# Attention with relative positions: sums over keys left of the query moved from TensorE to ScalarE and GpSimd

## The reference, cut

```python
xn = layernorm(x)                          # x: (2, 2048, 256)
q, k, v = proj(Wq, bq), proj(Wk, bk), proj(Wv, bv)      # 16 heads of 16
idx = clip(r[None, :] - r[:, None], -128, 128) + 128
scores = (einsum('bhqd,bhkd->bhqk', q, k) + einsum('bhqd,qkd->bhqk', q, rel_k[idx])) / sqrt(16)
w = softmax(scores, axis=-1)
s = (einsum('bhqk,bhkd->bhqd', w, v) + einsum('bhqk,qkd->bhqd', w, rel_v[idx])) @ Wo.T + bo
logits = xn @ Wg + bg                      # 8 experts, the best one per token
y = gelu(xn @ W1[e]) @ W2[e]               # e = argmax(logits)
out = x + s * silu(y)
```

## Time and profile before

| | |
|---|---|
| median of three runs | 2635.67 us (2635.24 to 2641.53) |
| profiled execution, its own time | 2641.73 us |
| its span | 2640.0 us |
| TensorE matmul busy | 2420.9 us (92%) |
| VectorE busy | 1828.1 us (69%) |
| ScalarE busy | 1749.4 us (66%) |
| GpSimd busy | 884.5 us (34%) |
| mean granted TensorE clock | 0.973 |

### The profile page before, as it was taken

The page is one execution under the profiler, slowest core; times in us unless marked ns, Lnnn a source line. Parts: engine busy times, 40 slices in busy tenths (PEclk is TensorE's granted clock), DMA queues, the critical chain, the costliest instruction groups (busy, mean ns, idle before and its releaser), DMA issues. The chain is left out here.

```text
span 2640.0 us, 47807 instructions
## 1 busy us (share of the span) xinstructions
PE 2420.9 (92%) x15216; PEld 1184.1 (45%) x15216; DVE 1828.1 (69%) x4985; ACT 1749.4 (66%) x4026; POOL 884.5 (34%) x1977
## 2 busy tenths in 40 slices
PE   6838999999999999999999999999999999799998
PEld 3412444444444444444444444444444444567666
DVE  6558777777777777777777777777777774233333
ACT  4514877777777777777777777777777777321121
POOL 1222454333333333333333333333333332133332
PEclk9955999999999999999999999999999999999999
DMA  5668889777777777777777777777777762642221
GB/s 160 176 141 265 244 268 243 235 222 230 233 230 237 225 222 233 234 231 236 232 228 234 231 236 236 231 226 226 233 231 238 227 194 88 244 144 69 66 64 53
DMA packets 351151, 541.00 MB, mean 205 GB/s; under 512 B 30608, under 2 KB 259392, under 8 KB 350912
## 3 DMA queue, kind: packets, MB, share of 16 engines
q1 hardware_dynamic: 336880, 502.76, 61.8%
q0 software_dynamic: 14032, 35.24, 4.5%
HBM read 272.60 MB, written 269.43 MB: 205 GB/s over the span
## 5 line engine op out<-in xcount | busy, mean ns | idle before, releaser
L1073 DVE TENSOR_REDUCE part<-ps 128x1 f32<-128x512 f32 (+3 forms) x2048 | 1189.5, 591 | 457.8 <-PE ps L957 438.8
L1135 ACT ACTIVATE probs_T<-pst 128x512 f32<-128x512 f32 (+3 forms) x2048 | 985.3, 525 | 397.4 <-PE pst L966 390.0
L957 PE MATMUL ps<-k_front,q_front 96*128 96x512 bf16 x2048 | 790.1, 393 | 13.0 <-DVE part L1071 2.5
L915 PE MATMUL pout<-probs_T,v_far 128*32 128x512 f32 (+3 forms) x4864 | 550.8, 533 | 40.4 <-ACT probs_T L1111 31.4
L822 POOL TENSOR_TENSOR left_T<-probs_T,left_mask 128x128 f32<-128x128 f32 x512 | 219.5, 429 | 991.7 <-ACT probs_T L1111 797.4
L957 PEld LDWEIGHTS ps<-k_front,q_front 96*128 96x128 bf16 x2048 | 198.6, 97 | 587.8 <-DVE part L1073 296.8
L966 PE MATMUL pst<-q_back,k_left 102*128 102x512 bf16 (+3 forms) x1024 | 349.7, 343 | 0.7 <-ACT probs_T L1135 0.6
L966 PE MATMUL pst<-q_back,k_right 102*128 102x512 bf16 (+3 forms) x1024 | 348.8, 342 | 0.5
L1148 ACT ACTIVATE band<-band,negm 128x384 f32<-128x384 f32 (+1 forms) x512 | 305.5, 597 | 0.1
L1071 DVE CUSTOM_DVE_ANT_0 band<-ps,band 128x256 f32<-128x256 f32 (+2 forms) x704 | 300.5, 427 | 0.0
L915 PEld LDWEIGHTS pout<-probs_T,v_far 128*32 128x32 f32 x4864 | 174.5, 108 | 237.9 <-issue 211.4
(11 more groups left out here) (160 smaller groups left out, 2112.0 us busy)
## 6 DMA issues: line engine op xcount, KB each, us to landing
rel_scores<-rel SPq DMA_DIRECT2D x128, 1024.0 KB, 7.9
band_probs<-band SPq DMA_DIRECT2D x128, 768.0 KB, 3.9
pwin<-band_probs SPq DMA_DIRECT2D x128, 512.0 KB
band<-rel_scores SPq DMA_DIRECT2D x64, 768.0 KB
band<-rel_scores SPq DMA_DIRECT2D x64, 576.0 KB, 5.2
w<-in_w_dram SPq DMA_DIRECT2D x16, 1024.0 KB, 14.3
band<-rel_scores SPq DMA_DIRECT2D x64, 128.0 KB, 5.7
q_terms<-terms SPq DMA_DIRECT2D x48, 128.0 KB
```

The source lines that it names most:

```text
L915: return nc.tensor.matmul(pout[32 * g:32 * g + 32, c0:c1], values, probs, start=first, stop=False, skip_group_check=True)
L957: nc.tensor.matmul(ps1[u % 2][:, :], q_front[a.par][:, a.s * P:(a.s + 1) * P], k_front[a.par][:, u * CW:(u + 1) * CW], start=True, stop=Tr ...
L1073: ins = nc.vector.tensor_reduce(peak, src, AX_X, ALU.max)
L1135: ins = nc.scalar.activation(probs_T[t.s % 2][:, u * CW + c0:u * CW + c1], pst[u % 2][:, c0:c1], ACT.Exp, scale=SCALE)
```

## The change

The sum over keys left of the query within its own block needs no product on TensorE: it is the sum of a masked row times one vector. The new kernel takes the diagonal block of `band`, with queries on partitions, masks it on GpSimd (lag 6), sums each row on ScalarE with a copy that accumulates (lag 7, at the step's end), multiplies the 16 sums of a pair by `rv_left` on GpSimd, and VectorE adds the product before the division. `left_T`, `left_values` and `all_pv` go. The shift rows are turned by VectorE in blocks of 32x32 into `shT` (lag 5, behind tile u=3) and placed into `q_back` by four copies on GpSimd; TensorE's transposes and ScalarE's copy go. The slots' indirect transfers move to the last 16 steps of the last head, two a step, and SP reads the table behind its loop.

```diff
-        left_T = sb("left_T", [P, NB, P], F32)
...
+        left = two("left", [P, P], F32)
+        left_sum = two("left_sum", [P, NB], F32)
+        left_part = two("left_part", [P, NB, HD], F32)
...
+        shb = two("shb", [P, CH, 32], BF16)
+        shT = sb("shT", [P, CH, 32], BF16)
...
-                    if hb == 2 and off == 2:
-                        sp.wait_ge(slots_filled, 16 * TILES)
-                        sp.dma_start(slots[:, :, :], dram["slots"].rearrange("(t p) k -> p t k", p=P)).then_inc(slots_in, 16)
...
+                sp.wait_ge(slots_filled, 16 * TILES)
+                sp.dma_start(slots[:, :, :], dram["slots"].rearrange("(t p) k -> p t k", p=P)).then_inc(slots_in, 16)
...
+                    q = Step(hb, off - 6)
+                    if off % CH == 2 and q.valid:
+                        pool.wait_ge(rows_tp, q.count(4, q.r + 1))
+                        if q.r == 0:
+                            wait(pool, st_mm, q.count(64, -64))
...
+                        summed = Step(hb, off - 7)
+                        if summed.valid:
+                            pool.wait_ge(left_ready, summed.count(16, summed.s + 1))
...
+                        rows = q_back[q.par][ROWS:ALLROWS, q.r * CW:(q.r + 1) * CW].rearrange("p (g b c) -> p b g c", g=CH, b=P // 32)
+                        for b in range(P // 32):
+                            if b > 0:
+                                pool.wait_ge(rows_link, q.count(12, 3 * q.r + b))
+                            ins = nc.gpsimd.tensor_copy(rows[:, b], shT[32 * b:32 * b + SHIFTS, :, :])
+                            ins.then_inc(rows_link if b < P // 32 - 1 else rows_copied, 1)
+                        pool.wait_ge(rows_copied, q.count(4, q.r + 1))
...
+                    w = Step(hb, off - 6)
...
-                        pool.wait_ge(bandT_evac, w.count(16, w.s + 1))
-                        if w.s == 0:
-                            wait(pool, all_pv, w.count(1, 0))
-                        own = probs_T[w.s % 2][:, w.s * P:(w.s + 1) * P]
-                        nc.gpsimd.tensor_tensor(left_T[:, w.s, :], own, left_mask[:, :], ALU.mult).then_inc(left_ready, 1)
+                        pool.wait_ge(band_ready, w.count(16, w.s + 1))
+                        own = band[w.par][:, w.s, P:2 * P]
+                        wait(pool, left_sums, w.count(16, w.s - 1))
+                        nc.gpsimd.tensor_tensor(left[w.s % 2][:, :], own, left_mask[:, :], ALU.mult).then_inc(left_ready, 1)
...
+                    ended = Step(hb, off - 8)
+                    if ended.valid and ended.s == NB - 1:
+                        pool.wait_ge(left_sums, ended.count(16, 16))
+                        wait(pool, norm_done, ended.count(1, -1))
+                        nc.gpsimd.tensor_tensor(left_part[ended.par][:, :, :], left_sum[ended.par][:, :].unsqueeze(2).to_broadcast([P, NB, HD]),
+                                                rv_left[:, :].unsqueeze(1).to_broadcast([P, NB, HD]), ALU.mult).then_inc(left_done, 1)
...
+                    first = 2 * NB + 3
+                    if at_end(hb) and first <= off < first + TILES // 2:
+                        if off == first:
                             pool.wait_ge(slots_set, 16)
-                        pool.indirect_dma_start(out=dram["slots"][:, :], out_offset=bass.IndirectOffsetOnAxis(ap=pos_i[:, off:off + 1], axis=0),
-                                                in_=tok_i[:, off, :], in_offset=None).then_inc(slots_filled, 16)
+                        for k in range(2):
+                            i = 2 * (off - first) + k
+                            pool.indirect_dma_start(out=dram["slots"][:, :], out_offset=bass.IndirectOffsetOnAxis(ap=pos_i[:, i:i + 1], axis=0),
+                                                    in_=tok_i[:, i, :], in_offset=None).then_inc(slots_filled, 16)
...
-                        pe.wait_ge(shift_ready, y.count(4, y.r + 1))
-                        wait(pe, rows_copied, y.count(4, y.r))
-                        if w.valid:
-                            wait(pe, winT_evac, w.count(16, w.s + 1))
-                        for g in range(CH):
-                            mm = nc.tensor.transpose(prow[0:SHIFTS, g * P:(g + 1) * P], shb[y.r % 2][:, g, :], con["ident_bf"][:, :])
-                        mm.then_inc(rows_tp, 1)
...
-                    def left_values():
-                        for g in range(CH):
-                            mm = weighted(g, 0, CW, rv_left[:, :], left_T[:, CH * g:CH * g + CH, :].rearrange("p i c -> p (i c)"))
-                        return mm
...
-                        if u == 0 and ended.s == NB - 1 and ended.valid:
-                            pe.wait_ge(left_ready, ended.count(16, 16))
-                            left_values().then_inc(all_pv, 1)
...
-                        if u == 1 and off % CH == 2 and y.valid:
-                            shift_rows()
...
-                        if off % CH == 2 and y.valid:
-                            pe.wait_ge(rows_copied, y.count(4, y.r + 1))
...
+                    def shift_rows():
+                        dve.wait_ge(shift_ready, shifted.count(4, shifted.r + 1))
+                        wait(dve, rows_copied, shifted.count(4, shifted.r))
+                        nc.vector.transpose(shT[:, :, :].rearrange("p g k -> p (g k)"), shb[shifted.r % 2][:, :, :].rearrange("p g k -> p (g k)")).then_inc(rows_tp, 1)
...
+                        if u == CH - 1 and off % CH == 1 and shifted.valid:
+                            shift_rows()
...
-                        dve.wait_ge(den_ready, o.count(1, 1))
                         dst = attn[:, o.n, :, :].rearrange("p (g r) d -> p r g d", g=CH)
-                        nc.vector.tensor_tensor(dst, back[:, :, :, 0:HD], rv.unsqueeze(3).to_broadcast([P, CH, CH, HD]), ALU.mult).then_inc(norm_done, 1)
+                        dve.wait_ge(left_done, o.count(1, 1))
+                        nc.vector.tensor_tensor(dst, back[:, :, :, 0:HD], left_part[o.par][:, :, :].rearrange("p (g r) d -> p r g d", g=CH),
+                                                ALU.add).then_inc(den_ready, 1)
+                        dve.wait_ge(den_ready, o.count(2, 2))
+                        nc.vector.tensor_tensor(dst, dst, rv.unsqueeze(3).to_broadcast([P, CH, CH, HD]), ALU.mult).then_inc(norm_done, 1)
...
-                        act.wait_ge(all_pv, ended.count(1, 1))
+                        act.wait_ge(near_pv, ended.count(2, 2))
...
-                    def shift_rows():
-                        act.wait_ge(rows_tp, shifted.count(4, shifted.r + 1))
-                        nc.scalar.activation(q_back[shifted.par][ROWS:ALLROWS, shifted.r * CW:(shifted.r + 1) * CW], prow, ACT.Copy).then_inc(rows_copied, 1)
...
-                        wait(act, left_ready, t.count(16, t.s - 1))
...
-                        if u == 1 and off % CH == 2 and shifted.valid:
-                            shift_rows()
...
+                    masked = Step(hb, off - 7)
+                    if masked.valid:
+                        act.wait_ge(left_ready, masked.count(16, masked.s + 1))
+                        if masked.s == 0:
+                            wait(act, left_done, masked.count(1, -1))
+                        own = left[masked.s % 2][:, :]
+                        nc.scalar.activation(own, own, ACT.Copy, accum_out=left_sum[masked.par][:, masked.s:masked.s + 1]).then_inc(left_sums, 1)
```

More of the change, by code:

```diff
@@ L555, in attend @@
         rv_win = sb("rv_win", [P, 2, 32], F32)
-        rv_left = sb("rv_left", [P, 32], F32)
+        rv_left = sb("rv_left", [P, HD], F32)
         part = sb("part", [P, NB, 3, CH], F32)
@@ L563, in attend @@
         sh = sb("sh", [P, CH, 2], F32)
-        shb = two("shb", [P, CH, SHIFTS], BF16)
+        shb = two("shb", [P, CH, 32], BF16)
+        shT = sb("shT", [P, CH, 32], BF16)
         rden = sb("rden", [P, NB], F32)
@@ L605, in attend @@
         rows_tp = sem("rows_tp")
+        rows_link = sem("rows_link")
         rows_copied = sem("rows_copied")
@@ L618, in attend @@
         near_pv = sem("near_pv")
-        all_pv = sem("all_pv")
+        left_sums = sem("left_sums")
+        left_done = sem("left_done")
         out_evac = sem("out_evac")
@@ L683, in near_columns @@
             return bl[0] * P, (bl[-1] + 1) * P
-        CONSTS = 18
+        CONSTS = 19
         with nc.Block() as block:
@@ L739, in step @@
                         wait(sp, bandT_mm, x.count(16, min(4 * r + 5, NB) - 32))
+                        wait(sp, left_ready, x.count(16, 4 * r + 4 - 32))
                         wait(sp, prob_out[r], x.count(16, -16))
@@ L788, in _ @@
                     pool.memset(rel_ends[p][:, :, :], 0.0).then_inc(const_set, 1)
+                    pool.memset(shb[p][:, :, :], 0.0).then_inc(const_set, 1)
                     pool.memset(rel[p][:, :, 0:1], 0.0).then_inc(const_set, 1)
@@ L801, in _ @@
```

(32 more changed lines are left out.)

5 lines of the change are left out of this document (removed).

## The result

The changed kernel takes 2693.89 us (median of 4 runs, 2690.67 to 2698.38) against 2635.48 for the kernel before (4 runs, 2635.24 to 2641.53): ratio 1.0217, 95% interval 1.0195 to 1.024. The profiled execution took 2696.09 us on a span of 2694.4, 54.4 more than the span of before. The forecast was 2700.

A forecast was written before the change was run, and what follows sets the result against it. It took a closed loop through ScalarE's near_keys and TensorE's value products as the bound. Loop +54 and slots +11 gave +65 on a span of 2640.0, 2700 us against the median; range 2610 to 2760.

The forecast's parts named there:

- The bound: Attention loop: a closed loop through ScalarE, whose near_keys releases TensorE's value products 0.14 us later, sets the step.
- Rival 2: Attention loop: TensorE is the bound, so everything taken from it counts, 3.4 us a pair; 2543 us, chance 0.06.
- The price M: Cost of ScalarE's masked-sum copy in 15 of 16 loop steps: 0.33 us, 0.25 copy plus 0.08 accumulator read; break-even 0.21.
- Rival 1: ScalarE's sum copy is nearly free in the loop, M = 0.16, -0.8 us a pair; 2622 us, chance 0.11.
- rival 3: ScalarE's accumulator read is dear, M 0.45 to 0.58, +3.6 to +5.5 us a pair; 2756 to 2816 us, chance 0.12.
- What was won: Work taken off TensorE: 3.2 us a pair, of which 2.13 in the four steps with shift_rows.
- the 1.07 of the rest: TensorE's other wins a pair: 0.37 us of spare in ordinary steps, 0.7 us from dropping left_values.
- The loop sum: Attention loop: 15 x 0.33 - 3.2 = +1.75 us a pair, over 30.8 pairs +54 us.
- VectorE and GpSimd: Their new transposes, added sum and row copies count 0, at most 0.2 us a pair (6 us).
- rival 4: GpSimd's row copies come late and hold TensorE's fourth tile, 0.9 us a pair; 2728 us, chance 0.05.
- The slots: End of attention: SP's late 11.4 us table read ends the stage, +9 us, plus 2 for seven more loop steps.
- Signs that were named: New trace: near_keys waits some 50 us in 500, pair 65.2 us, ScalarE over 85% busy, stage ending with the slots' read.

The follow-up runs named there:

- no_read: The changed kernel with ScalarE's copy of the masked probabilities without its accumulated sum; 2651.3 us, 63.00 us a pair.
- copy_twice: The changed kernel with one more 128x128 copy from SBUF on ScalarE ahead of the masked sum in each step; 2785.7 us, 67.32 us a pair.
- sum_in_gap: The changed kernel with ScalarE's masked sum moved from the step's end to behind the relative scores' copy (u=1); 2575.0 us, 60.55 us a pair.
- rows_only: The kernel before with only VectorE's block transposes and GpSimd's row copies for the shift rows, slots in mid-run; 2573.4 us, 61.10 us a pair.
- sums_only: The kernel before with only the left sums moved off TensorE, shift rows unchanged, slots in mid-run; 2705.5 us, 65.55 us a pair.

## Why the prediction was right, and where only the sum was

**The bound** held: in the new trace the products start 0.14 us after near_keys in ordinary steps, no_read and copy_twice moved the pair by what the loop gives for them, and sum_in_gap by 3.8 of its 4.35. Rival 2 (TensorE is the bound) is out by the time, and by sum_in_gap, in which the same TensorE work took 3.8 us a pair less.

**The price M** was taken as 0.33, 0.25 for the copy and 0.08 for the read. Measured: 0.20 and 0.09, so 0.29. The bound from the 512-wide copy (0.22 and more for the copy) was too high, the read's likeness to VectorE's (0.06 shown) was near. Rival 1 needed M below 0.19, rival 3 above 0.45. The Trainium skill's figure (VectorE: DVE Perf Modes, section "The TRN2 errata — SBUF-src ops pay a fixed extra latency per instruction", 0.29 us for the copy) agrees with the copy's duration, 303 ns; but the loop pays the 0.20 to its successor, and the sum that I made from the page, 2718, was 24 us too high.

**What was won**, 2.13 us of the four steps, is 2.30 by rows_only; the 1.07 of the rest is 1.04 by sums_only, if the sum is paid in 11 steps there (11 x 0.29 - 2.15). The loop sum with the measured M is 15 x 0.29 - 3.34 = +1.0 a pair, measured +0.94. The forecast had +1.75, so +54 us over the loop where the trace has +31 (29.6 and 1.7). The mis-sized term is M, 0.04 x 15 = 0.6 of these 0.8; the wins were 0.14 larger than counted.

**VectorE and GpSimd** at nothing held. The block transpose takes 303 ns where I took 0.2 within 0.083 to 0.42, the four row copies 1.34 us where I allowed 2, and in the step after the pair's end they end 1.8 us before TensorE's fourth tile (1019.00), so rival 4 did not come:

```profile
1015.89 1.34 POOL L841 COPY q_back<-shT 6x128 bf16<-6x128 bf16 x4 [0.16 <-POOL rel L889]
```

**The slots** are the step that failed. It said that SP's read of the table ends the stage, +9 us, with TensorE done by then. The stage ended with VectorE's product after a stall of all compute engines, +25, and the table's read, 5.3 us and not 11.4, was long over. I had read that the same transfers cost nothing in mid-run and had taken it for a property of the transfers; it was one of how they are issued. The two errors, -23 in the loop and +14 at the end (25.4 against 9 + 2), cancelled most of each other, so that +54.4 on the span came out beside +65: that the total is better than its parts is luck.

**Signs that were named:** the waits for near_keys grew to 33 us and not to some 50, ScalarE's share is 81% and not over 85%, the pair 64.3 and not 65.2. Only the pair follows from the smaller M: 0.04 us in 15 steps of 7.8 pairs is 5 us in 500, where the waits are 17 short and ScalarE's share 20; no run shows the rest. The last sign, the stage ending with the slots' read, did not come.

## What to carry to other kernels

An instruction on the engine that closes a loop costs the distance to its successor if it stands between the last input and the release, and little or nothing where that engine waits anyway: before moving work to ScalarE, look for the gap in its timeline, and put the work there. The change was worth +0.94 or -2.85 us a pair by the place of two instructions. And transfers that GpSimd issues indirectly belong in small groups with time to land between them, as far as these runs go; a place at the end, where nobody else needs GpSimd, lets them run in one row. Last, a cost that is read in one place (transfers one a step) holds for that spacing only.

## What the runs showed of the hardware

A row of 16 or 24 indirect transfers of 128x2 words, issued by GpSimd 1.26 us apart, made the stretch 14 and 26 us longer, with 1.8% of the DMA engines' time taken by their queue (with 24). The updates of TensorE's semaphores came up to 7 and 12 us late in it, and ScalarE and VectorE stood waiting for them. 24 plain ones issued 0.53 us apart did nothing of the kind, nor did the indirect ones with one in flight. TensorE's granted clock fell to 0.50 in it, and stayed there for some 6 us of the work after the stall. On ScalarE, the read of the accumulator lasts 195 ns and a 128x128 copy from SBUF 303, but their successors start after 0.09 and 0.20 us.
